# Four heads' negated row maxima turned in one set of four transposes, as twelve rows shared by the heads, with another table of attention tasks

## The reference

```python
Q = proj(query, wq_w, wq_b); K = proj(key, wk_w, wk_b); V = proj(value, wv_w, wv_b)   # 16 heads of 16
scores = jnp.einsum('bhqd,bhkd->bhqk', Q, K) * scale
scores = jnp.where(causal, scores, -jnp.inf)
attn = jax.nn.softmax(scores, axis=-1)
out = jnp.einsum('bhqk,bhkd->bhqd', attn, V)
...
x = _layernorm(x + attention(x, ctx))
...
vals, idx = jax.lax.top_k(logits.T, cap)          # experts choose their tokens
h = jax.nn.gelu(jnp.einsum('ecd,esdm->ecsm', xg, W1) + b1[:, None], approximate=False)
```

## Time and profile before

| | us |
|---|---|
| median of 3 runs | 695.46 (695.38 to 697.42) |
| profiled execution, its own time | 697.58 |
| its span, first to last instruction | 695.8 |
| attention, first turned maxima to the last exponentials | about 199.5 to 445 |
| PE busy in all | 602.1 (87% of the span) |

### The profile page before, as it was taken

One profiled execution on the slowest core, in us unless ns is written; L12 is line 12 of the kernel. 1 busy time (PEld: TensorE's weight loads), 2 busy tenths in 40 slices (PEclk: granted clock), 3 DMA queues, 4 the chain that ended last, 5 costly groups with the idle time before them and its releaser, 6 DMA issues.

```text
span 695.8 us, 11431 instructions
## 1 busy us (share of the span) xinstructions
PE 602.1 (87%) x4046; PEld 346.9 (50%) x4046; DVE 360.7 (52%) x791; ACT 275.7 (40%) x455; POOL 191.9 (28%) x250
## 2 busy tenths in 40 slices
PE   7999999999989889999999988930599999999945
PEld 3648576664754446555555554410145454554522
DVE  5843635143175665776587665279433333333535
ACT  3160421415036656666766567100043323333204
POOL 2333214050221131123123212110235445443214
PEclk9999999999999999999999999975699999999976
DMA  8794000011630631273045521066089999998655
GB/s 268 237 379 167 0 0 0 1 61 39 192 103 2 193 99 42 76 231 88 1 132 158 206 112 63 0 259 296 23 307 388 397 393 404 400 397 279 170 170 209
DMA packets 43566, 120.80 MB, mean 174 GB/s; under 512 B 6096, under 2 KB 28288, under 8 KB 40448
## 3 DMA queue, kind: packets, MB, share of 16 engines
q1 hardware_dynamic: 37936, 113.18, 45.1%
q0 software_dynamic: 4608, 6.29, 4.4%
q10 hardware_dynamic: 976, 0.73, 0.5%
...
## 4 chain that ended last, share of the span: by engine, by line
PE 76%; DVE 12%; ACT 4%; issue 3%; DMA 3%; POOL 1%; SPq 0%; ACTq 0%; POOLq 0%; DVEq 0%
PE PS L1910 12%; PE PS L1588 8%; PE PS L1597 8%; PE PS L1745 5%; PE PS L1758 5%; PE PS L1676 4%; PE PS L1942 4%; PE PS L1717 4%; PE PS L1923 3%; DVE Mx L1053 3%; PE PS L1695 2%; PE PS L1936 2%; PE PS L1559 2%; PE PS L1576 2%; PE PS L1713 2%
## 5 line engine op out<-in xcount | busy, mean ns | idle before, releaser
L1053 DVE TENSOR_REDUCE Mx<-PS 128x1 f32<-128x384 f32 (+3 forms) x176 | 102.8, 634 | 52.2 <-PE PS L1717 51.7
L1418 ACT ACTIVATE arena<-PS 128x512 f32<-128x512 f32 (+1 forms) x176 | 90.6, 560 | 47.1 <-PE PS L1745 45.6
L757 POOL TENSOR_SCALAR_AFFINE_SELECT arena<-arena 128x512 f32<-128x512 f32 x64 | 41.0, 640 | 176.6 <-ACT arena L1418 176.6
L1745 PE MATMUL PS<-arena 99*128 99x512 bf16 (+3 forms) x256 | 61.9, 304 | 11.3 <-ACT arena L1418 10.2
L1717 PE MATMUL PS<-arena 96*128 96x128 bf16 (+3 forms) x256 | 62.3, 301 | 0.0
L1588 PE MATMUL PS<-arena 128*128 128x512 f32 x128 | 56.1, 593 | 3.2 <-ACT arena L1327 1.6
L1597 PE MATMUL PS<-arena 128*128 128x256 f32 x256 | 55.9, 379 | 0.0
L1490 ACT ACTIVATE X<-X 128x512 f32<-128x512 f32 x48 | 29.4, 630 | 62.4 <-DVE X L1238 62.4
L1597 PEld LDWEIGHTS PS<-arena 128*128 128x128 f32 x256 | 48.6, 190 | 6.5
L1231 DVE COPY X<-PS 128x512 f32<-128x512 f32 x24 | 16.6, 691 | 67.5 <-PE PS L1910 67.5
L1758 PE MATMUL PS<-arena 128*32 128x128 f32 (+3 forms) x512 | 48.5, 449 | 1.2 <-POOL arena L757 1.0
...
...
## 6 DMA issues: line engine op xcount, KB each, us to landing
...
arena<-pieces SPq DMA_DIRECT2D x192, 64.0 KB, 2.3
...
```

The costliest lines, as they stand in the source:

```text
L757: pool.affine_select(out=pb[j % 2][:, :, 0:P], in_=pb[j % 2][:, :, 0:P], compare_op=ALU.is_ge, fill=0.0, base=0, pattern=[[0, GH], [1, P]] ...
L1053: dve.tensor_reduce(Mx[:, g % 2, i, heads[0]:heads[-1] + 1], bank(score_banks[(g * NSH + u) % 3])[:, 0:len(heads) * w] .rearrange("p (h n) ...
L1418: act.activation(pb[j % 2][:, heads[0]:heads[-1] + 1, 0:w], bank(exp_banks[(g * NSH + n) % 2])[:, 0:len(heads) * w] .rearrange("p (h n) -> ...
L1745: mm = pe.matmul(bank(exp_banks[(g * NSH + n) % 2])[:, a * w:(a + 1) * w], KTs[0:SX, g * GH + h, j * P:(j + 1) * P], QTs[0:SX, g * GH + h, ...
```

## The change

Instead of eight transposes of 128x3 for each pair of heads, one transpose of 128x12 is made for each tile of queries: the three pieces of all four heads of the group in twelve rows. It is four transposes in bank 5 instead of sixteen in banks 5 and 7. Every head's QTs gets all twelve rows, its own and those of the three other heads; ACT still makes two copies, now of 12x(2x512), each from the same 512 columns of bank 5, repeated for two heads. So that a head adds only its own maximum, KTs no longer has ones in all of these rows, but ones in the head's own three rows and zeros in the nine others: `own`, made once by DVE from the identity matrix, is spread by four POOL copies of 12x2048 in place of four memsets of 3x2048.

```diff
-SX = SK + NPC
+SX = SK + GH * NPC
...
-CUTS = [(3, 3), (4, 4), (3, 4), (0, 0)]
+CUTS = [(3, 3), (4, 4), (3, 3), (0, 0)]
...
-    (0, 0): ([("value", 1, 0)], [], [], []),
+    (0, 0): ([("query_in", 0, 1), ("query_in", 1, 1)], [], [], []),
...
+        own = sb("own", [P, GH])
...
+            pool.wait_ge(owns, 1)
...
-                pool.memset(KTs[SK:SX, GH * g:GH * g + GH, :], 1.0).then_inc(ones, 1)
+                pool.tensor_copy(KTs[SK:SX, GH * g:GH * g + GH, :],
+                                 own[SK:SX, :].unsqueeze(2).to_broadcast([SX - SK, GH, T]))\
+                    .then_inc(ones, 1)
...
+            dve.tensor_reduce(own[SK:SX, :], ident[SK:SX, SK:SX]
+                              .rearrange("p (h c) -> p h c", h=GH), AX.X, ALU.add)\
+                .then_inc(owns, 1)
...
+                act.wait_ge(ntp.s, ntp.now(b, g + 1))
                 for m in range(2):
-                    act.wait_ge(ntp.s, ntp.now(b, 2 * g + m + 1))
                     act.activation(QTs[SK:SX, GH * g + 2 * m:GH * g + 2 * m + 2, :],
-                                   spare(m).bitcast(BF16)[SK:SX, :]
-                                   .rearrange("p (h n) -> p h n", h=2), ACT.Copy)\
+                                   wide(spare(0).bitcast(BF16)[SK:SX, 0:T], 2), ACT.Copy)\
                         .then_inc(nte.s, 1)
...
-                for m in range(2):
-                    o = take(m, nte, nte.now(b, 2 * g + m + 1)).bitcast(BF16)
-                    for h in range(2):
-                        for i in range(TT):
-                            mm = pe.transpose(o[SK:SX, (TT * h + i) * P:(TT * h + i + 1) * P],
-                                              nst[:, g % 2, i, 2 * m + h, :], identb[:])
-                    mm.then_inc(ntp.s, 1)
+                o = take(0, nte, nte.now(b, 2 * g + 2)).bitcast(BF16)
+                for i in range(TT):
+                    mm = pe.transpose(o[SK:SX, i * P:(i + 1) * P],
+                                      nst[:, g % 2, i].rearrange("p h c -> p (h c)"), identb[:])
+                mm.then_inc(ntp.s, 1)
```

27 lines of the change are left out of this document (14 added, 13 removed).

## The result

The changed kernel took 690.32 us in the median of 8 runs (689.88 to 694.46), the kernel before 695.42 beside it. The medians lie 5.1 us apart where 11.7 were forecast; the ratio of the means is 0.9937 (95% interval 0.9913 to 0.996), which is 4.4 us. The time lies in the range, at its upper end, and outside the likeliest case's own range. The profiled execution took 690.3 us, its span is 688.6, which is 7.28 less than the span of before.

A forecast was written before the change was run, and what follows sets the result against it. PE was taken to bound attention, with ACT setting the pace at group starts without a PE task. Gains of 5.3 (two middle images), 3.15 (first) and 3.25 (last) sum to 11.7: 685.9 profiled, 683.8 us median; range 675.0 to 690.5.

The forecast's parts named there:

- the likeliest case: Whole kernel: tasks in gaps and fewer transposes give 683.8 us, by itself from 679 to 688.5; chance 0.56.
- the middle images: Second and third image in attention: 2.65 us gained in each, 5.3 for two, idle time moved rather than removed.
- the ones: POOL's copies in place of memsets, before attention: hidden until PE's first transposes end, so nothing; without that cover up to 5.8.
- the keys: Keys through memory to the next image's first scores: ready with 2.4 us left, so nothing counted.
- the first image: First image in attention: 3.15 us gained in all, after a loss of 1.75 for `value` 1 ahead of all slots.
- the last image: Last image in attention, without tasks for a next one: 3.25 us gained, 2.1 of it in group 3 from `logits`.
- CUTS: Last scores behind value products: PE's 0.2 us wait filled, last maximum 0.15 to 0.25 later, net nothing.
- that subtraction: Whole kernel: 685.9 for the profiled execution less 2.12, by which the median of the runs was lower, gives 683.8 us.
- ACT keeps the pace: Rival, attention: only 0.22 us gained in each group (3.5), about 2 at the last `logits`, 690; chance 0.17.
- The gaps are really filled: Rival, attention: half of PE's 19.4 us idle time goes besides 10.8 of transposes, 675.0; chance 0.15.
- no change: Rival, attention: ACT's copies take 1.5 us each and eat the gain of 11.7, 695.5; chance 0.06.
- the keys come too late: Rival, next image's first scores: PE waits for key reads, 700 us at 5.5 beyond the 2.4 left; chance 0.06.

The follow-up runs named there:

- the idle matmuls: The changed kernel with 6, 6 and 11 useless matmuls ahead of PE's wait for `nst` at three places, against the kernel before: 689.30 us, ratio 0.9908.
- the rows alone: The twelve shared rows with TASKS and CUTS of before, everything else as in the change, against the kernel before: 696.18 us, ratio 1.0004.

## Why the prediction was right in part and missed

**Right: the middle images.** Forecast 59.9 us for an image, measured 59.70. Group by group of the third: 15.24, 16.8, 14.5, 13.3 forecast, 14.93, 17.06, 14.22, 13.49 measured. The four are off by 0.2 to 0.3 us each in both directions, so the sum is closer than its parts. The third bank stands at T + 3.61 in group 0 and at 4.54, 4.36, 4.34 in the others. The only wait for `nst` is at the end of group 2 (0.93), where DVE is busy 13.50 of 14.22. That the idle time is moved and not removed held as well for such an image (3.6 us of PE before, 3.5 after). Right too: the price of `value` 1 ahead of all slots (1.88 for 1.75), of the copies (1.93 for 1.92), of the ones (nothing), and the keys: sent out 1.86 behind T, no PE wait on a DMA.

**Wrong: the first image** (-4.9 forecast without the prologue, -1.17 measured), the largest miss with 3.7 us. Group 0 gained 1.67 for 1.3 and group 3 lost 0.30 for 0.5. Two steps failed.
- Group 1: "about 1.2 of it stays, and `key` 0 goes into the gap: gain 3.1"; 1.15 came. The gap was filled, but PE's idle time in the group fell by 0.76 only: part of the freed time went into waits for ACT's copies (0.57) and for maxima (0.53), and 1.81 of the wait for `nst` stayed. I had counted that wait as caused by `split_k` alone. It is a chain of last scores, their maximum and `negate`, which PE's earlier arrival only meets sooner, with the CAST held by POOL's select for 0.39.
- Group 2: "gains 1.0 from `value` 0 in the gap"; it lost 1.35. The stretch at the lower clock costs 1.35, as the idle matmuls show, and the group is then as long as before (14.22). Of the 1.0 that is missing even so, 0.7 is in the wait at its end, which grew from 1.09 to 1.80. The clock had no term in the sum, and the wait had none for this group.

**Wrong: the last image** (-3.25 forecast, -1.94 measured). The step "Group 0 loses `value` 1 (gain 1.0)" overlooked POOL's `bias`, which the new table puts into slot (0, 2), beside `negate`, in a group that has no `query` to cover it: it lost 0.32, and with `bias` elsewhere it gains 0.82. The low clock behind that wait took 0.6 in group 1. Group 2 gained nothing for 0.35, with its wait for `nst` at 0.93 for 0.54. The last group gained 2.9 where 2.1 were forecast; the profile of before has a stretch at half the clock there (433.9 to 437.4), so a part of this gain is probably luck.

**Mis-sized: CUTS.** "Net nothing" is a loss of about 0.8 us in attention: the maximum is later, and the CAST is held by the select.

**The offset.** The two profiled executions lie 7.28 us apart, the medians 5.1. The profile of before lies 2.16 above its median, the one of after on its median. So 4.4 us of the miss are in the steps above. The other 2.2 are in that subtraction, which took what the profiled execution of before had beyond its median as if the changed kernel had it too. I assume that it is stretches at the lower clock; no profile of a median execution of before is there to show it.

**The rivals.** "ACT keeps the pace" gave the time (690), and 0.22 us for a group, 0.88 for an image, is near what the rows alone gave with the old table (0.84). That the sums agree is partly luck, as its groups gained 0.35, 0.06, 0.21 and 0.22, and its time for the whole change is luck too. For the whole change its mechanism is wrong: PE, not ACT, sets the third bank in three groups of four. "The gaps are really filled", "no change" (copies of 1.5 us) and "the keys come too late" show nowhere.
